# Convolution taps folded into TensorE's products, and the skip term D times u added through a diagonal, in a Mamba and attention kernel

## The reference, cut to what matters

```python
xz = jnp.einsum('bsd,ed->bse', xn, in_proj_w)
x_in, z = jnp.split(xz, 2, axis=-1)
xt = jnp.transpose(x_in, (0, 2, 1))
u = conv(xt, conv_w)          # depthwise, causal, D_CONV = 4 taps, DI = 512 channels
u = jax.nn.silu(transpose(u + conv_b))
x_dbl = jnp.einsum('bsd,ed->bse', u, x_proj_w)
dt_r, B, C = jnp.split(x_dbl, [DT_RANK, DT_RANK + N], axis=-1)
dt = softplus(dt_r @ dt_proj_w.T + dt_proj_b)
# for each time step: h = h * exp(dt * A) + (dt * u) * B ;  y = sum over n of h * C
y = ys + u * D_param
y = y * jax.nn.silu(z)
out = jnp.einsum('bsd,ed->bse', y, out_proj_w)
```

## Time and profile before

| | |
|---|---|
| median of 3 runs | 570.05 us (568.83 to 570.15) |
| profiled execution, its own time | 569.01 us |
| its span | 567.2 us |
| busy: VectorE | 514.6 us (91%) |
| busy: GpSimd | 453.0 us (80%) |
| busy: TensorE matmul | 437.9 us (77%) |
| busy: ScalarE | 408.6 us (72%) |
| mean granted TensorE clock | 0.901 of full |

### The profile page before, as it was taken

How to read it: one execution, slowest core, us unless ns; L and a number is a source line. 1 busy time by engine, 2 the same in 40 slices (tenths; PEclk the granted TensorE clock), 3 DMA queues, 4 the chain that set the end, 5 groups by cost and what they waited for, 6 DMA issues and landing times. The chain is left out here.

```text
span 567.2 us, 7391 instructions
## 1 busy us (share of the span) xinstructions
PE 437.9 (77%) x2456; PEld 361.2 (64%) x2456; DVE 514.6 (91%) x566; ACT 408.6 (72%) x897; POOL 453.0 (80%) x318
## 2 busy tenths in 40 slices
PE   8967666769789787768688678768787777866887
PEld 7646445657676676656576667647674666755776
DVE  2479899999999999999999999999999999999753
ACT  2693677668865998578966999488966988486533
POOL 4049969989998889979998889978997989985121
PEclk8988777896789798998989898998899898779899
DMA  9294032201430044001440045011440045000001
GB/s 269 66 326 125 3 114 85 102 4 54 159 112 0 29 151 154 14 19 40 159 131 1 28 151 165 2 29 43 147 129 1 10 151 166 2 0 20 0 1 37
DMA packets 22366, 45.38 MB, mean 80 GB/s; under 512 B 3685, under 2 KB 13557, under 8 KB 22329
## 3 DMA queue, kind: packets, MB, share of 16 engines
q1 hardware_dynamic: 22328, 44.92, 24.3%
HBM read 42.52 MB, written 2.39 MB: 79 GB/s over the span
## 5 line engine op out<-in xcount | busy, mean ns | idle before, releaser
L530 POOL TENSOR_TENSOR hs<-dtu,Br 128x1024 f32<-128x1024 f32 x127 | 297.0, 2362 | 8.5 <-DMA Br<-bc_rows 8.5
L722 ACT ACTIVATE ring<-dt,Aneg 128x256 f32<-128x256 f32 x512 | 212.9, 465 | 72.6 <-DVE hs L957 68.7
L950 DVE TENSOR_TENSOR_SCAN ring<-ring,hs 128x1024 f32<-128x1024 f32 x97 | 221.4, 2282 | 5.8 <-ACT ring L722 5.4
L1298 PE MATMUL sums<-ident,hs 128*128 128x128 f32 x1024 | 150.7, 303 | 36.3 <-DVE hs L957 36.0
L1298 PEld LDWEIGHTS sums<-ident,hs 128*128 128x128 f32 x1024 | 134.4, 158 | 48.3 <-DVE hs L957 44.7
L957 DVE TENSOR_TENSOR hs<-ring,Cr 128x1024 f32<-128x1024 f32 x97 | 118.8, 1225 | 3.3
L539 POOL TENSOR_TENSOR hs<-hs,Cr 128x1024 f32<-128x1024 f32 x31 | 73.2, 2360 | 42.1 <-DVE hs L950 42.1
L950 DVE TENSOR_TENSOR_SCAN hs<-ring,hs 128x1024 f32<-128x1024 f32 x31 | 70.3, 2269 | 0.0
L1366 PE MATMUL PY<-wqkvo,xT 128*128 128x256 f32 x168 | 46.6, 428 | 0.0
L1293 PE MATMUL sums<-ident,uD 128*128 128x128 f32 x64 | 15.5, 333 | 35.2 <-DVE ygT L964 35.2
L1366 PEld LDWEIGHTS PY<-wqkvo,xT 128*128 128x128 f32 x168 | 37.5, 223 | 6.6
(11 more groups left out here) (218 smaller groups left out, 694.1 us busy)
## 6 DMA issues: line engine op xcount, KB each, us to landing
Br<-bc_rows SPq DMA_DIRECT2D x32, 512.0 KB, 5.1
Cr<-bc_rows SPq DMA_DIRECT2D x32, 512.0 KB, 4.2
xg<-in_x SPq DMA_DIRECT2D x8, 256.0 KB, 2.9
out<-fin SPq DMA_DIRECT2D x7, 256.0 KB, 4.2
hs<-in_ada_wT SPq DMA_DIRECT2D x3, 512.0 KB, 4.6
win<-in_in_wT SPq DMA_DIRECT2D x2, 512.0 KB, 6.1
hs<-in_W_emb SPq DMA_DIRECT2D x2, 512.0 KB
gate<-gate_rows SPq DMA_DIRECT2D x8, 128.0 KB, 3.1
```

Source lines behind the costliest of these rows:

```text
L530: nc.gpsimd.tensor_tensor(hs[:, g % DBUF], dtu[:, b % 2, dc, :].unsqueeze(1).to_broadcast([P, NQ, T]), Br[:, NQ * q:NQ * q + NQ, :], ALU.m ...
L722: ins = nc.scalar.activation(ring[:, g % 2, j, :], dt[:, b % 2, dc, :], ACT.Exp, scale=Aneg[:, c:c + 1])
L950: V.tensor_tensor_scan(driven if by_pool(g) else decays, decays, driven, 0.0, ALU.mult, ALU.add).then_inc(s_scan_done, 1)
L1298: ins = M(YT[:, c, :], hs[:, g % DBUF, j, P * c:P * c + P], ident[:, :], is_transpose=True, start=False, stop=(q == UPC - 1 and j == NQ - ...
```

## The change

For batches 1 to 7 and h = 1 (channel groups 2 and 3) the taps are folded: the weights are scaled by each of the four taps once at the start, and `in_proj` adds the four taps' products in PSUM, the moving side shifted by s columns. `conv_last_tap` then only adds the bias (scale 1), and `conv_taps` is skipped. Batch 0 and h = 0 stay as they were. The skip term no longer passes ScalarE: TensorE multiplies u with diag(D), built once on GpSimd. The waits are recounted, as `taps_until` and `wait_x_read` below do.

```diff
+FOLDED = (1,)
+FOLD_LO, FOLD_N = 2 * P * FOLDED[0], 2 * P * len(FOLDED)
+def folded(b, h):
+    return b >= 1 and h in FOLDED
+def taps_until(b, h):
+    return sum(3 * 2 for c in range(b + 1) for k in range(2) if not folded(c, k) and (c, k) <= (b, h))
...
+        wtap = sb("wtap", [P, TAPS - 1, KD, FOLD_N])
-        uD = sb("uD", [P, 2, T])
+        diagD = sb("diagD", [P, DC, P])
+        wrow = hs[:, 1:1 + len(FOLDED)].rearrange("p s n t -> p (s n t)").rearrange("p (s e) -> p s e", s=TAPS)
...
+            sp.dma_start(wrow, a["tap_rows"][:, FOLD_LO:FOLD_LO + FOLD_N].unsqueeze(0).to_broadcast([P, TAPS, FOLD_N])).then_inc(
+                s_ld_taps, 16)
             broadcast_bc(0)
...
+            def diagonals():
+                pool.wait_ge(s_ld_par, 32)
+                pool.wait_ge(s_ld_ident, 16)
+                for dc in range(DC):
+                    nc.gpsimd.tensor_scalar(diagD[:, dc, :], ident[:, :], pcol("D_par", dc, dc + 1), None,
+                                            ALU.mult).then_inc(s_diag_ready, 1)
+            def scale_taps():
+                pool.wait_ge(s_ld_taps, 16)
+                pool.wait_ge(s_xz_mm, 2)
+                part = win[:, :, FOLD_LO:FOLD_LO + FOLD_N]
+                for s in range(1, TAPS):
+                    nc.gpsimd.tensor_tensor(wtap[:, s - 1], part, wrow[:, s, :].unsqueeze(1).to_broadcast([P, KD, FOLD_N]),
+                                            ALU.mult).then_inc(s_taps_ready, 1)
+                pool.wait_ge(s_taps_ready, TAPS - 1)
+                nc.gpsimd.tensor_tensor(part, part, wrow[:, 0, :].unsqueeze(1).to_broadcast([P, KD, FOLD_N]),
+                                        ALU.mult).then_inc(s_taps_ready, 1)
+                pool.wait_ge(s_taps_ready, TAPS)
             for g in range(FIRST, LAST):
+                if g == -6:
+                    diagonals()
+                    scale_taps()
...
                 for e in range(2):
                     dc = 2 * h + e
+                    tap = 1.0 if folded(b, h) else pcol("conv_w", TAPS * dc + 3, TAPS * dc + 4)
...
             def silu_u(b):
-                act.wait_ge(s_tap_done, 3 * DC * (b + 1))
+                act.wait_ge(s_conv0_ready, DC * (b + 1))
+                act.wait_ge(s_tap_done, taps_until(b, 1))
                 if b >= 2:
-                    act.wait_ge(s_uD_ready, DC * (b - 1))
+                    act.wait_ge(s_y_acc, U * (b - 1))
...
-            def skip_term(b, dc):
-                if DC * b + dc >= 2:
-                    act.wait_ge(s_uD_added, DC * b + dc - 1)
-                nc.scalar.activation(uD[:, dc % 2, :], u[:, b % 2, dc, :], ACT.Copy,
-                                     scale=pcol("D_par", dc, dc + 1)).then_inc(s_uD_ready, 1)
...
             def conv_taps(b, h):
+                if folded(b, h):
+                    return
...
+            def wait_x_read(b, h):
+                pe.wait_ge(s_conv0_ready, DC * b + 2 * h + 2)
+                if not folded(b, h):
+                    pe.wait_ge(s_tap_done, taps_until(b, h))
             def in_proj(b, h):
...
                     if h >= 2:
-                        pe.wait_ge(s_tap_done, 3 * DC * b + 6 * (h - 1))
+                        wait_x_read(b, h - 2)
                 elif h <= 2:
-                    pe.wait_ge(s_tap_done, 3 * DC * b + 6 * h)
+                    wait_x_read(b, h - 1)
...
+                if h < 2 and folded(b, h):
+                    if b == 1:
+                        pe.wait_ge(s_taps_ready, TAPS)
+                    for e in range(2):
+                        lo = P * (2 * h + e)
+                        bank = xz_bank(b, h)
+                        for s in range(TAPS):
+                            for k in range(KD):
+                                w = wtap[:, s - 1, k, lo - FOLD_LO:lo - FOLD_LO + P] if s else win[:, k, lo:lo + P]
+                                ins = M(bank[:, e, s:T], w, xnT[:, k, 0:T - s], start=(s == 0 and k == 0),
+                                        stop=(s == TAPS - 1 and k == KD - 1), skip_group_check=True)
...
             def sum_states(b, i):
...
                 if q == 0:
-                    pe.wait_ge(s_uD_ready, DC * b + dc + 1)
+                    pe.wait_ge(s_u_ready, b + 1)
+                    if g == 0:
+                        pe.wait_ge(s_diag_ready, DC)
                     if DC * b + dc >= 1:
                         pe.wait_ge(s_ygT_ready, DC * b + dc)
                     for c in range(TC):
-                        ins = M(YT[:, c, :], uD[:, dc % 2, P * c:P * c + P], ident[:, :], is_transpose=True,
-                                start=(c == 0), stop=False, skip_group_check=True)
-                    ins.then_inc(s_uD_added, 1)
+                        M(YT[:, c, :], u[:, b % 2, dc, P * c:P * c + P], diagD[:, dc, :], start=(c == 0), stop=False,
+                          skip_group_check=True)
```

More of the change, by code:

```diff
@@ L204, in build @@
         s_ld_post = sem("ld_post")
+        s_ld_taps = sem("ld_taps")
+        s_taps_ready = sem("taps_ready")
+        s_diag_ready = sem("diag_ready")
         s_pool_const = sem("pool_const")
@@ L256, in build @@
         s_ygT_ready = sem("ygT_ready")
-        s_uD_ready = sem("uD_ready")
-        s_uD_added = sem("uD_added")
         s_yback_mm = sem("yback_mm")
@@ L614, in conv_last_tap @@
                     dc = 2 * h + e
+                    tap = 1.0 if folded(b, h) else pcol("conv_w", TAPS * dc + 3, TAPS * dc + 4)
                     nc.scalar.activation(conv[:, dc, :], xz_bank(b, h)[:, e, :], ACT.Identity, bias=pcol("conv_b", dc, dc + 1),
-                                         scale=pcol("conv_w", TAPS * dc + 3, TAPS * dc + 4)).then_inc(s_conv0_ready, 1)
+                                         scale=tap).then_inc(s_conv0_ready, 1)
             def copy_z(b):
@@ L864, in _ @@
                     softplus_second()
[L865 to L868, removed]
                 if g == LAST_B * U + 14:
@@ L913, in conv_taps @@
                         if s > 1:
-                            dve.wait_ge(s_tap_done, 3 * DC * b + 6 * h + 2 * (s - 2) + e + 1)
+                            dve.wait_ge(s_tap_done, taps_until(b, h) - 6 + 2 * (s - 2) + e + 1)
                         w = pcol("conv_w", TAPS * dc + 3 - s, TAPS * dc + 4 - s)
@@ L1232, in in_proj @@
                     if h >= 2:
-                        pe.wait_ge(s_tap_done, 3 * DC * b + 6 * (h - 1))
+                        wait_x_read(b, h - 2)
                 elif h <= 2:
-                    pe.wait_ge(s_tap_done, 3 * DC * b + 6 * h)
+                    wait_x_read(b, h - 1)
                 else:
                     pe.wait_ge(s_z_ready, 3 * b + 1)
-                if h < 2:
+                if h < 2 and folded(b, h):
[9 more added lines that the diff above has]
+                                        stop=(s == TAPS - 1 and k == KD - 1), skip_group_check=True)
+                elif h < 2:
                     for e in range(2):
@@ L1595 @@
         "ada_b": L0_cond_ada_b, "in_wT": np.asarray(L0_cond_in_proj_w).T, "xp_wT": np.asarray(L0_cond_x_proj_w).T,
+        "tap_rows": np.asarray(L0_cond_conv_w).reshape(DI, TAPS).T[::-1],
         "dt_wT": np.asarray(L0_cond_dt_proj_w).T, "dt_b": L0_cond_dt_proj_b, "out_wT": np.asarray(L0_cond_out_proj_w).T, "Wq": L1_cond_Wq,
```

## The result

| | before | changed |
|---|---|---|
| median | 569.73 us (4 runs) | 587.52 us (4 runs, 585.49 to 590.32) |
| ratio | | 1.0318, 95% interval 1.0267 to 1.0369 |
| span of the profiled execution | 567.2 us | 587.1 us |
| mean granted TensorE clock | 0.901 | 0.910 |

What follows compares the result with a forecast made beforehand. VectorE, busy 91%, was held to be paced by ScalarE's exponentials, queued behind TensorE's folded products. Boundaries 18.7, batch 1 0.5, opening 0.2, skip term -0.5: +18.9 on 569.0, 587.9; half of 1.0 added, 588.5 us; range 579 to 598.

Steps and rivals of the forecast that it cites:

- the chain at the boundaries: Batches 2 to 7: longer TensorE products delay ScalarE's copies, exponentials and VectorE's scan of unit 3; 18.7 us lost in sum.
- Relief of VectorE: Taps off VectorE in seven batches: 2.42 us a batch, 16.9 us won if the exponentials were in time.
- Folded products: TensorE's in_proj(b, 1): 32 records take 6.92 us where eight took 1.73, 5.19 us more, ahead of ScalarE's copies.
- Ordinary boundary: Scan of unit 3 around batches 4, 6 and 7: VectorE gives up 2.42 us, waits 4.97, so 2.55 us lost each.
- The other boundaries: Batches 3 and 5, whose chain starts later, lose 3.68 us each; batch 2, at TensorE's lower clock level, loses 3.64.
- Batch 1: Folded part ahead of the setup products delays sums and gate by 2.0 us; +0.5 taken, ends -1.4 and +2.0.
- The opening: GpSimd's four weight scalings before the scale of batch 1, a step without slack: +0.2 us taken, ends 0 and +2.
- the open point: The new 512 KB load in the opening: each microsecond it lands after 19.94 adds one.
- Backlog of TensorE: Sums of unit 3 done by 376.00, gate needs them at 376.03: fits only just, no further wait counted.
- Diagonal: Skip term on TensorE: two more records, 0.22 us a group, 7 us in all; only unit 0's adds to the chain.
- The rule on transposes and the clock: Transposes do not count for TensorE's clock gate as other matmuls do, so the change would keep the clock up.
- The rival that the prediction put beside it (583.1): The clock stays up: all six boundaries lose 2.55 us, batch 1 is at -1.4, +13.6 in all; chance 17%.

Runs made afterwards that it cites:

- fold_only: The changed kernel with the skip term scaled by ScalarE and transposed as before, no diagonal, so the folded taps alone: 585.53 us, ratio 1.0283.
- no_taps: The changed kernel with the three shifted taps' products left out for the folded groups, output incomplete: 559.53 us, ratio 0.9826.
- act_order: The changed kernel with, from batch 2 on, ScalarE's copies of folded products and copy_yg moved behind the exponentials of units 3 and 4: 582.37 us, ratio 1.0218.

## Why the prediction was right

588.5 us was forecast and 587.52 measured. The forecast was the chain at the boundaries, and fold_only, no_taps and act_order show it from three sides. The mechanism was right; that the number came within 1 us is in part luck, as two of the steps show. Step by step:

- *Relief of VectorE.* 2.42 us a batch. Shown: without any products in its place the kernel is 9 us faster (no_taps). That is less than 16.9, and as much as was expected of that run, but its trace puts the parts elsewhere. The scans of unit 3 at the six boundaries gain 14.7 us against those of unit 0, batches 2, 3 and 5 as much as the others or more, where 12.3 was expected. Behind unit 3, 5.5 of this is lost again, 3.7 of it at the gate, which waits for TensorE's sums (2.70 once, 0.25 four times). The first scan came 3.2 us later than before (37.14 against 33.95). The sign that VectorE's busy time would fall by 20 us was misreckoned from the mean of 472 ns for 42 instructions: these overlap, six of them take 2.42 us, and it fell by 16.2.
- *Folded products.* 5.19 us more was forecast; 6.87 - 1.73 = 5.14 measured.
- *Ordinary boundary.* 2.55 us lost was forecast; 4.58 - 2.42 = 2.16 measured. Of the 0.4 between them 0.18 is ScalarE's shorter copies and 0.05 the products. The rest is in how the relief is read: the six instructions last 2.42 us, but what follows them started 2.34 behind their start, and where nothing held it the scan started 0.08 before the end of the statistics, from which the wait of 4.58 is counted. Read from start to start (scan of unit 0 to scan of unit 3), 18.60 against 16.28, the loss is 2.32, and 0.18 and 0.05 are all that is missing.
- *The other boundaries.* 3.64, 3.68 and 2.55 for batches 2, 3 and 4, and 3.68 for 5; measured 1.65, 5.12, 4.83 and 2.16. Here the step was wrong in where, not in the sum: the lower level of the clock was carried over from the batches where the trace of before had it. In the changed kernel it fell into the sums and the first folded products of batches 3 and 4, and spared 2 and 5. The sum over six is 18.1, for 18.7. That it agrees is luck: two boundaries came out 2.0 and 1.5 us below the forecast, two others 1.4 and 2.3 above it.
- *Batch 1.* +0.5 was taken, with an upper end of 2.0; from the first scan to that of unit 6 the changed kernel needs 2.1 us more. Reckoned from the first scan, the gate comes 3.5 us later than before (58.66 - 32.85 against 56.25 - 33.95), where 2.0 was taken. The other 1.5 is that in_proj(1, 0) already starts 1.6 us later (37.17 - 32.85 against 36.68 - 33.95). The products behind the gate did run at the full level and gave 1.5 back: 1.72 us from the start of one to the next, 3.24 before. The sums of units 0 to 3 gave nothing back, though of the 3.8 us of idle time behind them 0.6 was left:

```profile
53.30 5.32 PE L1349 MATMUL sums<-ident,hs 128*128 128x128 f32 x32
```

From 54 to 57 us the granted clock was 0.50, with TensorE busy all the time, as it was from 48 to 50 us in the trace of before. In both traces these sums come right behind the products with eight columns.
- *The opening.* +0.2 was taken, with an upper end of 2; it lost 1.6. This does not show in the span of this execution: up to ScalarE's first copy it ran 2.7 us ahead of that of before (15.57 against 18.26), with a granted clock of 1.00 between 8 and 13 us against 0.70, and 1.1 of that was left at the first scan (32.85 against 33.95). What gives the opening one level or the other is open. The loss is the late landing that had been named as the open point. The span grew by 19.9: 18.1 at the boundaries, 2.1 - 1.1 up to unit 6, and 0.8 in small differences elsewhere. So the total is luck here too: batch 1 and the opening together cost 3.7 us where 0.7 was taken, and the head start of 2.7 us hid most of the difference.
- *Backlog of TensorE.* Forecast to fit with almost nothing to spare; the gate at 391.75 did not wait, 0.7 us behind the end of the sums. act_order shows how near it was: this is what gave the gate its 3.9 us of wait.
- *Diagonal.* Its 0.22 us is right (0.24), but alone it costs some 2 us (1.0039), where it was thought to fit into the slack. Two boundaries of that kernel's trace have the lower level in the same chain, with VectorE's taps waiting 1.79 and 0.61 us; whether the diagonal brings this about was not tried.
- *The rule on transposes and the clock.* The rival that the prediction put beside it (583.1) did not come about: the changed kernel had more products and fewer transposes, and the lower level at two boundaries, where three had it before. The mean clock rose from 0.901 to 0.910 only. One run does not speak against the rule; it gave nothing here.

## What to carry to other kernels

Work taken off the busiest engine is won only if the inputs of its next step are there; look at which in-order queue they stand in, and what that queue waits for. Here an independent piece of work (the exponentials) stood behind a wait that had used up its slack, and 5 us more in front of that wait cost more than the 2.4 us that were taken off VectorE. When such a wait is removed, look for the next one before measuring: here there were three in a row (ScalarE's copies, TensorE's output projection, gate_x), and only the first two together turned an 18 us loss into equality.

## What the runs showed that was not expected

- The lower clock level lies in other places from kernel to kernel. In the changed kernel's windows (length, busy PE, PEld, DVE, ACT, POOL, granted clock, DMA, GB/s) where batch 4 is prepared, TensorE is idle for a good half of the first stretch and busy after it, is granted half the clock in both, and all of it later:

```profile
238.00:240.00 2.00, 0.75 (x3) 0.75 (x4) 2.00 (x6) 0.00 (x0) 2.00 (x2) 0.50 0.00 0
240.00:242.00 2.00, 2.00 (x12) 2.00 (x11) 2.00 (x2) 0.00 (x0) 1.05 (x2) 0.50 0.00 0
...
246.00:248.00 2.00, 2.00 (x11) 1.78 (x10) 0.46 (x3) 0.00 (x0) 2.00 (x2) 1.00 0.01 4
```

It costs the scan 7.25 - 4.58 = 2.7 us, more than the 1.7 forecast for such a spell, since it covers the sums ahead too.

- ScalarE's copy from PSUM with the constant scale 1.0 takes less time than with a scale per partition: two take 0.84 us where they took 1.02.
- A late load shows only where the opening is early. The tap rows landed at 20.6 in the changed kernel (12.1 and 8.5 us) and in act_order alike. In the first ScalarE had started its copies of batch 0 at 15.57, and later waited 3.39 us for the scale of batch 1; in act_order it started them at 19.00 and did not wait.
